# Attention, mixture of experts and convolution in one kernel: the next values in step 15, tokens in step 1, the last batch's routing at other steps, the last outputs of the first pass in bank 7

## What is computed

```python
# experts: 8 experts, hidden 256, the best two of each token
logits = xf @ Wg + bg
w, idx = top_k(softmax(logits), 2);  comb = one_hot(idx) * w / sum(w)
h = relu(einsum('nd,edh->enh', xf, W1) + b1)
y = einsum('enh,ehd->end', h, W2) + b2
out = einsum('end,ne->nd', y, comb)
# attention: 4 query sets share keys and values; 16 heads of 8; causal
att = softmax(where(causal, q_g @ k.T / sqrt(8), -inf))
out = concat(att_g @ v over g) @ W_proj.T

x = x + conv(layernorm(x));  x = x + experts(layernorm(x))
x = x + attention(layernorm(x));  x = x + experts(layernorm(x))
```

## Time and profile before

| | us |
|---|---|
| median of 3 runs | 876.06 (874.88 to 877.28) |
| the profiled execution's own time | 874.92 |
| its span, from the first to the last instruction | 873.2 |
| mean granted TensorE clock, as a share of 2.4 GHz | 0.992 |
| TensorE busy | 825.0 |
| ScalarE busy | 727.7 |
| VectorE busy | 657.1 |
| GpSimd busy | 549.7 |

### The profile page before, as it was taken

The page is one execution under the profiler, slowest core; times in us unless marked ns, Lnnn a source line. Parts: engine busy times, 40 slices in busy tenths (PEclk is TensorE's granted clock), DMA queues, the critical chain, the costliest instruction groups (busy, mean ns, idle before and its releaser), DMA issues.

```text
span 873.2 us, 20943 instructions
## 1 busy us (share of the span) xinstructions
PE 825.0 (94%) x7953; PEld 465.6 (53%) x7953; DVE 657.1 (75%) x1966; ACT 727.7 (83%) x918; POOL 549.7 (63%) x620
## 2 busy tenths in 40 slices
PE   5899999999999899999999999999989999999995
PEld 4644577777777433333333333333223777777774
DVE  6898689988987566777777777777565888777775
ACT  7630588888898799999999999999997788988884
POOL 1177455555543688888888888888885454444432
PEclk9999999999999899999999999999999999999999
DMA  8101100000003334434444433355300000000000
GB/s 282 33 1 48 49 2 2 2 2 2 2 16 84 98 82 92 85 93 83 98 90 98 90 83 85 96 99 98 97 1 2 2 14 14 14 14 13 14 14 15
DMA packets 38408, 46.00 MB, mean 53 GB/s; under 512 B 6680, under 2 KB 24352, under 8 KB 38304
## 3 DMA queue, kind: packets, MB, share of 16 engines
q1 hardware_dynamic: 38304, 44.62, 21.5%
HBM read 27.83 MB, written 16.78 MB: 51 GB/s over the span
## 4 chain that ended last, share of the span: by engine, by line
PE 69%; DVE 13%; ACT 10%; issue 4%; POOL 2%; SPq 0%; DMA 0%; ACTq 0%
PE psum L766 18%; PE psum L718 17%; PE psum L1064 13%; ACT prob L1022 7%; PE psum L1013 5%; PE psum L1119 4%; DVE normed L341 3%; PE psum L545 2%; POOL prob L1037 2%; ACT decay L409 2%; PE psum L906 2%; DVE o_tok L1072 2%; PE psum L691 2%; PE psum L616 1%; PE psum L512 1%
## 5 line engine op out<-in xcount | busy, mean ns | idle before, releaser
L1022 ACT ACTIVATE prob<-psum 128x1536 f32<-128x1536 f32 x256 | 349.7, 1474 | 26.7 <-PE psum L1013 26.7
L1064 PE MATMUL psum<-prob,vstack 128*32 128x256 f32 (+1 forms) x2048 | 206.9, 499 | 2.6 <-DVE o_tok L1072 2.6
L718 PE MATMUL psum<-xt_parts,w_parts 128*128 128x512 f16 x768 | 186.8, 379 | 0.0
L778 DVE SCALAR_TENSOR_TENSOR mixed<-psum,comb_y,mixed 128x128 f32<-128x128 f32 x512 | 143.5, 342 | 2.1 <-PE psum L766 2.1
L748 POOL TENSOR_TENSOR hidden_parts_second<-hidden_second,hidden_parts_second 128x512 f16<-128x512 f32 x64 | 78.0, 1219 | 104.5 <-ACT hidden_parts_second L734 104.5
L748 POOL TENSOR_TENSOR hidden_parts_first<-hidden_first,hidden_parts_first 128x512 f16<-128x512 f32 x64 | 80.0, 1253 | 82.6 <-ACT hidden_parts_first L734 82.6
L732 ACT ACTIVATE hidden_first<-psum,b 128x512 f32<-128x512 f32 x128 | 88.2, 689 | 26.7 <-PE psum L718 19.1
L1032 POOL TENSOR_SCALAR_AFFINE_SELECT prob<-prob 128x512 f32<-128x512 f32 x128 | 82.4, 644 | 43.7 <-ACT prob L1022 38.3
L732 ACT ACTIVATE hidden_second<-psum,b 128x512 f32<-128x512 f32 x128 | 88.4, 691 | 25.2 <-PE psum L718 23.8
L1013 PEld LDWEIGHTS psum<-qstack,kstack 32*128 32x128 f16 x768 | 24.8, 91 | 157.0 <-ACT prob L1022 117.2
L1013 PE MATMUL psum<-qstack,kstack 32*128 32x512 f16 x768 | 100.9, 390 | 8.0 <-POOL prob L1037 3.6
(11 more groups left out here) (116 smaller groups left out, 1110.2 us busy)
## 6 DMA issues: line engine op xcount, KB each, us to landing
qstack<-qk_parts SPq DMA_DIRECT2D x128, 128.0 KB, 3.6
qk_parts<-parts SPq DMA_DIRECT2D x64, 192.0 KB, 3.2
kstack<-qk_parts SPq DMA_DIRECT2D x128, 32.0 KB, 3.6
stream<-L_attn_a_u SPq DMA_DIRECT2D x4, 512.0 KB, 7.5
kept_x<-stream SPq DMA_DIRECT2D x4, 512.0 KB, 2.6
out<-mixed SPq DMA_DIRECT2D x8, 256.0 KB, 2.3
w_whole<-L_ffn_W SPq DMA_DIRECT2D x1, 1024.0 KB, 7.4
taps<-c_taps SPq DMA_DIRECT2D x1, 640.0 KB, 8.4
```

Source lines behind the costliest of these rows:

```text
L718: last = e.matmul(bank(u % 4), m.w1[:, w_part, ex, cols], xt_parts[:, s, x_part, :], start=(n == 0), stop=(n == len(PRODUCTS) - 1))
L778: last = e.scalar_tensor_tensor(out=m.y[:, t0 + t, :], in0=bank(4 + i % 2)[:, t * P:(t + 1) * P], scalar=comb_y[:, s, t, ex:ex + 1], in1=m ...
L1022: e.activation(prob[:, n % PROBS, :], psum[:, TILE * (n % 2):TILE * (n % 2 + 1)], ACT.Exp, scale=SCALE)\
L1064: last = e.matmul(to[SLOT * lane:SLOT * (lane + 1)], vstack[:, b % 2, keys, first:first + SLOT], weights_of(n - t, lane, keys, pair), star ...
```

## The change

- In each batch the values of the next batch are computed (and copied by VectorE) in step 15 instead of 14, and the tokens of the batch after next are transposed (and cast) in step 1 instead of 0.
- In the last batch: the transpose of normed tokens goes from step 0 to 1, that of the routing weights from 8 to 12 (with the wait for the residuals of batch 14, before it at step 14), the two projections of batch 14 from 10 and 11 to 8 and 9, where they wait for the first step of the routing instead of its last copy; VectorE combines in step 8 instead of 6, ScalarE's copies follow.
- The last product of the first expert pass goes to bank 7 instead of 5, and waits for the base of the last chunk, which left bank 7. The scores of step 1 wait for 63 accumulations instead of 64; the first weighted sums, which use bank 7, wait for all 64.

```diff
--- before.py
+++ after.py
@@ -748,9 +748,13 @@
         e.tensor_tensor(m.hidden_parts[:, r, 1, 1, :], m.hidden[:, r, 1, :], m.hidden_parts[:, r, 0, 1, :],
                         ALU.subtract).then_inc(low_second, 1)
 
+    def down_bank(m, i):
+
+        return 7 if m is first and i == EXPERTS * FFN_CHUNKS - 1 else 4 + i % 2
+
     def tensor_down(e, m, ch, ex):
         i = (m.at + ch) * EXPERTS + ex
-        r, to = i % HRING, bank(4 + i % 2)
+        r, to = i % HRING, bank(down_bank(m, i))
         if m.whole:
             e.wait_ge(relued, HBLK * (i + 1))
             terms = [(m.hidden[:, r, k], m.w2[:, ex * HBLK + k, :]) for k in range(HBLK)]
@@ -761,6 +765,8 @@
                      for k in range(HBLK) for h_part, w_part in PRODUCTS]
         if i >= 2:
             e.wait_ge(accum, i - 1)
+        if down_bank(m, i) == 7:
+            e.wait_ge(based, FFN_CHUNKS)
         for t in range(FFN_TILES):
             for n, (h_, w_) in enumerate(terms):
                 last = e.matmul(to[:, t * P:(t + 1) * P], h_[:, t * P:(t + 1) * P], w_, start=(n == 0),
@@ -775,7 +781,7 @@
         else:
             e.wait_ge(accum, i)
         for t in range(FFN_TILES):
-            last = e.scalar_tensor_tensor(out=m.y[:, t0 + t, :], in0=bank(4 + i % 2)[:, t * P:(t + 1) * P],
+            last = e.scalar_tensor_tensor(out=m.y[:, t0 + t, :], in0=bank(down_bank(m, i))[:, t * P:(t + 1) * P],
                                           scalar=comb_y[:, s, t, ex:ex + 1], in1=m.y[:, t0 + t, :], op0=ALU.mult,
                                           op1=ALU.add)
         last.then_inc(accum, 1)
@@ -999,7 +1005,7 @@
         if n >= 2:
             e.wait_ge(exped, n - 1)
         elif n == 1:
-            e.wait_ge(accum, EXPERTS * FFN_CHUNKS)
+            e.wait_ge(accum, EXPERTS * FFN_CHUNKS - 1)
         else:
             e.wait_ge(relued, HBLK * EXPERTS * FFN_CHUNKS)
         if n % STEPS_B == 0:
@@ -1054,7 +1060,7 @@
         if n % STEPS_B == 0:
             e.wait_ge(v_copied, b + 1)
         if n == 0:
-            e.wait_ge(based, FFN_CHUNKS)
+            e.wait_ge(accum, EXPERTS * FFN_CHUNKS)
         elif t == 0:
             e.wait_ge(turned, n // 4)
         e.wait_ge(masked, n - t + needs + 1)
@@ -1112,7 +1118,8 @@
         elif b + 3 == BATCH:
             e.wait_ge(attn_done, HALVES * b + 1)
         elif b + 2 == BATCH:
-            e.wait_ge(combt_copied, FFN_CHUNKS + 1)
+
+            e.wait_ge(routed, STEPS * FFN_CHUNKS + 1)
         else:
             e.wait_ge(turned, BATCH * QUADS)
         for g in range(SETS):
@@ -1459,26 +1466,26 @@
     STARTS = [divmod(n, STEPS_B) for n in range(LAST)]
 
     def tensor_beside(e, b, at):
-        if b + 2 < BATCH and at == 0:
+        if b + 2 < BATCH and at == 1:
             tensor_at_x(e, b + 2)
         if b + 2 < BATCH and at in (4, 8, 12):
             tensor_qk(e, b + 2, at // 4 - 1)
         if 0 < b < BATCH - 1 and at in (7, 11):
             tensor_project(e, b - 1, at // 8)
-        if b + 1 < BATCH and at == 14:
+        if b + 1 < BATCH and at == 15:
             tensor_v(e, b + 1)
         if b + 1 == BATCH:
-            if at == 0:
+            if at == 1:
                 e.wait_ge(v_copied, BATCH)
                 tensor_xt(e, second, 0)
             elif at == 4:
                 tensor_logits(e, second, 0)
-            elif at == 8:
+            elif at in (8, 9):
+                tensor_project(e, b - 1, at - 8)
+            elif at == 12:
+                e.wait_ge(attn_done, HALVES * (BATCH - 1))
                 tensor_comb_t(e, second, 0)
-            elif at in (10, 11):
-                tensor_project(e, b - 1, at - 10)
             elif at == 14:
-                e.wait_ge(attn_done, HALVES * (BATCH - 1))
                 tensor_base(e, second, 0)
 
     def tensor_attention(e):
@@ -1497,15 +1504,15 @@
 
                 e.wait_ge(down_up, EXPERTS * FFN_CHUNKS)
             scalar_exp(e, n)
-            if n == LAST - STEPS_B:
+            if n == LAST - STEPS_B + 1:
                 scalar_xt(e, second, 0)
             elif n == LAST - STEPS_B + 5:
                 scalar_gap(e, second, 0)
-            elif n == LAST - STEPS_B + 8:
+            elif n == LAST - STEPS_B + 12:
                 scalar_comb_t(e, second, 0)
 
     def vector_beside(e, b, at):
-        if b + 2 < BATCH and at == 0:
+        if b + 2 < BATCH and at == 1:
             vector_at_x_high(e, b + 2)
             vector_at_x_low(e, b + 2)
         if b + 2 < BATCH and at in (4, 8, 12):
@@ -1539,7 +1547,7 @@
         if b + 1 == BATCH:
             if at == 4:
                 vector_top(e, second, 0)
-            elif at == 6:
+            elif at == 8:
                 vector_combine(e, second, 0)
             elif at == 14:
                 vector_base(e, second, 0)
```

## The result

The changed kernel takes 888.5 us (887.6 to 891.38, 4 runs) against 875.64 us for the kernel before (874.88 to 877.28, 4 runs). The ratio is 1.015, with a 95% interval of 1.0122 to 1.0178: slower by 1.5%. The profiled execution of the changed kernel took 891.38 us, at the upper end of its runs; its span is 889.6 us, 16.4 more than before.

The account below looks back on a forecast made before the run. ScalarE was taken to bound from step 15's exponentials to step 7's scores, TensorE from there to step 15. Boundaries +8.7, start -1.2 and last batch -1.0 made +6.5 us on the median 876.06: 882.5, range 875 to 889.

Parts of the forecast that it names:

- rival 3: TensorE's clock falls at the new stalls, some 1.7 us each, at five of thirteen boundaries +8: 891 us; chance 0.11.
- The old wait goes, 0.61: In each batch, TensorE's 0.61 us idle ahead of the next batch's values, waiting for VectorE's low parts, disappears.
- S(14): The scores of step 14 of a batch's 16 steps; S(n) stands for the scores of step n.
- The transpose starts 5.34 after S(14): Tokens' transpose in step 1 waits for VectorE's copy behind the turn: a new stall of 1.10 us, +0.91 a boundary.
- Given back from S(2) to S(7): Scores of step 2 to step 7: TensorE sets the pace instead of ScalarE, 6.41 for 6.72 us, so -0.31.
- Wait for the rows at step 7: The projection of step 7 waits for transposed rows: some 0.15 us, bounded by 0 and 0.3; summed as +0.16 a boundary.
- The boundaries into batches 1, 12 and 13: Batch boundaries reckoned apart from the ten ordinary ones: +0.58 into batch 1, +0.91 into 12, +0.12 out of 12.
- From 13 to 14: Boundary from batch 13 to 14: no transpose follows, so the gain stands alone, -0.53 us.
- The start, -1.2: Bank 7 for the last outputs lets batch 0's step 1 scores start earlier: -1.2 us, bounds 0.6 and 2.5 of gain.
- The last batch, -1.0: Last batch's routing: 1.56 us idle removed, a wait at step 12 added; taken -1.0, bounds -2.5 and +1.5.
- Rival 1: At the batch boundaries the copy comes soon enough, period 22.6 us, and the kernel gets faster: 867 us; chance 0.08.
- Rivals 1 and 2: The second: half of the boundary stall is hidden, leaving 0.5 to 0.7 us; about 876 us, no change; chance 0.09.

Follow-up runs that it names:

- copy first: The changed kernel with VectorE's copy of the values called ahead of the turn in step 15: 870.73 us against 876.26 for the kernel before.
- copy between: The changed kernel with VectorE's copy of the values between the turn's transpose and its two followers: 868.84 us against 875.95 for the kernel before.
- the filled kernel: The changed kernel with the score matmuls of step 1 of batches 1 to 13 each made three times: 886.07 us against 876.19 for the kernel before.

## Why the prediction was right in sign and half in size

The forecast was 882.5 us, +6.5; measured is 888.5, +12.9. That lies 0.5 us inside the stated range of 875 to 889, whose upper end had been stretched towards rival 3; by the forecast's own spread, 878 to 887, the time was outside, so there is some luck in it. The mechanism is the forecast one: the copy behind the turn, the transpose behind the copy, 13 times. Taking the wait away (copy first) and shortening the chain (copy between) both take the loss away. By its steps:

- *The old wait goes, 0.61.* Right: S(14) to S(15) takes 1.33, S(15) to S(0) 1.76 (forecast 1.33 and 1.77).
- *The transpose starts 5.34 after S(14).* It is 5.60. The step that was too small is the 1.63 for the turn with its followers, taken from the row of the kernel before: it is 1.82 now (508.75 to 510.57), because the multiplication of the turn (line 1083) takes 0.75 where it took 0.57. The turn started as forecast (3.22 after S(14), forecast 3.23), and the wake took 0.15, 0.09 more than I put. The transpose itself took 0.04 less. So a boundary costs 1.13 to S(2), not 0.91.
- *Given back from S(2) to S(7).* 0.34 (6.72 less 6.38), forecast 0.31.
- *Wait for the rows at step 7.* 0.18, forecast 0.16. Together 0.98 for an ordinary boundary, forecast 0.76: **2.2 us** of the miss over ten.
- *The boundaries into batches 1, 12 and 13.* Without stretches, as the filled kernel's trace has them, +1.02, +1.27 and +0.33; forecast +0.58, +0.91 and +0.12. Into batch 1, S(2) comes 1.02 later where I put 0.73, and the wait for the rows at step 7 is 0.34 where I put 0.16. The other two have the 0.22 of the ordinary boundary too little. Into batch 12 S(7) to S(8) takes 3.41 us in the changed kernel against 2.91 before (591.16 to 594.57), 0.50 more where 0.31 was put. Out of batch 12 the 0.65 of the old wait that was taken as gained was gained. Together **1.0 us**. From 13 to 14: -0.50, forecast -0.53.
- *The clock (rival 3).* Right as a mechanism and wrong as an alternative, with a chance of 0.11: it does not replace the forecast but adds to it, here at three of thirteen boundaries, 1.57 to 2.23 us each (I had put 1.7), **5.5 us** in the profiled execution, and 4.6 us in the second one, again at three. I had argued from idle times of 1.26 and 1.56 that did no harm. A boundary adds 0.48 and 1.25 within 2 us, and three cases could not show what happens in three of thirteen. What the Trainium skill says in "TensorE: Matmul & The Clock Gate", Part 1, that the half rate comes at moments the kernel does not set, agrees with two traces of one kernel that differ in place. Why these short idle times bring a fall in some batches and not in others stays open.
- *The start, -1.2.* -2.49 in the profiled execution, because its clock held; in the second one only -0.25, and -0.52 in the filled kernel. The bounds of -0.6 and -2.5 left these two out.
- *The last batch, -1.0.* +1.57 in this execution, beyond the bound of +1.5. I had put the transpose's wait for the last copy at 0. It is 1.16, a half-clock stretch follows it, and S(7) comes 0.78 later than before (15.30 us after S(14) of batch 14 against 14.52). Another half-clock stretch follows the 2.19 wait of the routing weights at step 12:

```profile
656.87 1.11 PE L591 MATMUL psum<-eye,normed 128*128 128x128 f32 x4 [1.16 <-DVE vstack L995]
657.92 1.94 PE L1070 MATMUL psum<-prob,vstack 128*32 128x512 f32 x8
...
676.97 0.69 PE L676 MATMUL psum<-eye,comb 128*8 128x128 f32 x4 [2.19 <-DVE stream L1136]
```

The second stretch is not there in the other two traces with this order of work, which have -0.63 (the changed kernel once more) and -0.64 (filled): S(7) comes as late, 15.29 and 15.28, but the wait at step 12 is 1.52 and the clock holds behind it. With the copy between turn and followers, where no stretch lies in the last batch, it is -1.12. So the forecast of -1.0 was near for a last batch with one stretch or none, and most of the +2.6 beyond it here is clock too:

```profile
678.45 0.60 PE L676 MATMUL psum<-eye,comb 128*8 128x128 f32 x4 [1.52 <-DVE stream L1136]
```

Profile against profile: 6.5 forecast, +2.2 for the ten boundaries, +1.0 for the odd ones, +5.5 for the clock at boundaries, -1.3 at the start, +2.6 in the last batch: 16.4 in all but for rounding, as measured. Against the median the miss is 6.0 (888.5 less 882.5), since the profiled execution was 2.9 us above it.

Rival 1 named the condition: it decides at a stall of 0.50 us. The copy between turn and followers, with 0.11, is faster than before, and the changed kernel, with 1.31, is slower, so the threshold lies between; nothing was run close to it. From the periods it is lower: with 22.82 at no stall, one to one, the old 23.13 is reached at about 0.31, an estimate. Rivals 1 and 2 left the wait for the rows out, 0.18 of this difference.

## What to carry to other kernels

When a producer is moved to a later slot, follow its consumer on each engine to where it stands in that engine's own order: the matmuls were moved behind their wait, and their copy fell behind a task that waits for work issued after them. The remedy was one place in VectorE's order, and it was worth some 18 us. A new idle time can also cost the clock: here a fall cost 1.4 to 2.2 us where the new idle time was 1.25. That the short idle time of 0.48 just ahead of it is needed for a fall was not tested.

## What was not expected of the hardware

The same VectorE multiplication mostly took 0.42, 0.57 or 0.75 us, by its place in the batch. VectorE and GpSimd side by side in the kernel before (0.57), and in the changed one (0.75):

```profile
456.00 0.57 DVE L1077 TENSOR_TENSOR o_norm<-o_tok,rden 128x256 f32<-128x256 f32 x1
...
455.42 0.87 POOL L1040 TENSOR_SCALAR_AFFINE_SELECT prob<-prob 128x768 f32<-128x768 f32 x1 [0.51 <-ACT prob L1022]
```

```profile
509.50 0.87 POOL L1046 TENSOR_SCALAR_AFFINE_SELECT prob<-prob 128x768 f32<-128x768 f32 x1
```

GpSimd's mask ends at 456.29 in the first, 0.29 into the multiplication, and at 510.37 in the second, 0.48 into it (509.89 to 510.37). The excess over 0.42 is 0.15 and 0.33. So the moved step changed what it overlaps, and that made the stall longer than its rows said. All twelve traces follow one pattern: in each of the 313 cases in the attention phase where a mask that was running at the multiplication's start had 0.27 us or more left, the multiplication ended 0.26 to 0.29 after the mask; in the 257 where GpSimd ran nothing at its start it took 0.42 or 0.43. The 1.07 in batch 13 belongs here too, with 0.80 of a mask left. This is read from traces alone; no run took the mask away. The Trainium skill, "GPSIMD Engine Reference", section "1. Specifications", says that GpSimd shares its SBUF interfaces with VectorE and contends with instructions that have two SBUF inputs, as this one has; the traces agree for the masks. In 54 cases GpSimd was at a small operation (128x4, line 335) instead, and the multiplication took 0.42 to 0.44, no longer than alone.

TensorE's clock in the same program fell at other places in two executions, with idle times equal to 0.01 us. Two more such stretches come and go: of the twelve traces, three have none at the start of attention and one has none in the last batch. The changed kernel's two traces differ by 2.2 us in each of these two places (20.92 against 18.68, and 31.26 against 29.06). Timed executions of one kernel differ by 1 to 7 us here; that these stretches make most of it is likely from these lengths, but not measured.
